# A four-layer graph network on one core: the second edge stage split in two, its larger part woven into the deep passes

## The chip, the cores and the metric

The kernel runs on one core of a Trainium2 chip. The metric is the device time of one execution in microseconds (us). The engines are TensorE (PE, with its weight loads PEld), VectorE (DVE), ScalarE (ACT), GpSimd (POOL) and SyncE (SP). Each has its own program, and they meet in semaphores. All gathers and scatters by index are issued by POOL; plain transfers are issued by SP or ACT.

## The reference

A graph has 100,000 nodes with 48 features and 50,000 edges, sorted by their destination `dst`. Four layers follow one another, each with a residual and a layernorm.

```python
x = _layernorm(x + L0(x))   # x + segment_sum(relu(x[src] + edge_attr), dst)
x = _layernorm(x + L1(x))   # ten times: f = 0.9 * segment_sum(f[src] * w, dst) + 0.1 * x
x = _layernorm(x + L2(x))   # relu(segment_sum(h2[src, type] * norm, dst) + bias2),
                            #   h2 = relu(x @ W1[r] + b1) @ W2[r], 8 relations r
x = _layernorm(x + L3(x))   # segment_max((x[dst]-x[src]) @ theta.T + theta_b + x[src] @ phi.T + phi_b, dst)
```

All is in float32. A node that no edge points to has a short way of its own, since its sums are zero.

## The kernel before, in words

Edges are worked on in groups of 512 (128 partitions by `T` = 4 columns). There are 100 groups (`NG`), taken four (`U`) to a turn, so 25 turns (`NT`). A running sum over a group of sorted edges is a scan by DVE on transposed data (`tensor_tensor_scan`, with a row of ones and zeros `kb` that restarts it at each new destination). PE makes the transposes.

Ten steps of layer 1 would need ten passes over all edges. The kernel follows chains instead: an edge whose source is nobody's destination ends there. "Level" lists hold the edges that still have a way to go, and they shrink: 40 groups at level 0, 20 at level 1, 10 at level 2. After that seven "deep" passes of ten groups each go on over the last list. Stages run one after the other, with a barrier between them. In the order of the trace they are: setup, counting and clearing, node stage, first edge stage, second edge stage, level 0, level 1, level 2, deep passes, sum stage, third-layer stage, fourth-layer stage.

**Second edge stage.** One group's work ("body") is a row of parts with lags: in step g the engines do layer 1's norm for group g (`norm2`), the relational product of group g−1 (`second`, `weigh` which gives `mw`, and two scans into `sc`: `add_up` and `highest`), layer 2's norm of group g−2 (`norm3`), and the last layer's norm of group g−3 (`norm4`, after the product by `thi` in `own`), whose rows POOL scatters to `out`. `part(work, i, s, lag, end)` places such a part; the order of the calls in a `body` is the order on the engine. The stage also writes `rt` (both scans' rows) into columns of `run_rows`, and SP copies `upper_rows` beside them. While it runs, POOL gathers for 44 of the groups (`listed=True`, 11 turns at most) the rows of parents (`fetch`) that level 0 needs, and SP stores them to `parent_rows`.

**Level 0** (`level(0, run_rows)`) gathers rows of 193 numbers from `run_rows` (the running sum's 97 and `rt`'s 96), computes with the first 97 and stores the other 96 to `held`, from which the third-layer stage reads later.

**Deep passes** (`steps`, function `one`). For each of ten groups: POOL gathers four times 128 rows of the last pass (`ugb`), DVE multiplies by the edge weight (`message`, `umsg`), PE transposes, DVE scans (`add_up`), PE transposes back, ACT copies to `rbuf` (`urb`), DVE adds that to a total kept in SBUF for all groups (`total_2`, printed as `total`), and SP stores `rbuf` for the next pass. In the first pass a second table, `fourth`, is added once. The last pass scales `rbuf` by ten, adds the total and scatters it to `deep_sum`. A pass can start its gathers only when the pass before has stored all of its rows. Engines know only each other's semaphores, so the deep list's count, read from memory, sets the trips of each loop.

**Sum stage.** For the 40 groups of level 0's list it adds `first_sum` and two `deep_sum` tables, does the norm, and stores to `layer[2]`. POOL has no part in it.

## Time and profile before

| | us |
|---|---|
| median of 3 runs | 4377.33 |
| lowest and highest run | 4374.49, 4379.94 |
| span of the profiled execution | 4361.2 |
| second edge stage, by the trace | 1376 to 2400 |
| level 0 | 2405 to 2670 |
| level 1 | 2690 to 2912 |
| level 2 | 2935 to 3005 |
| deep passes | 3010 to 3497 |
| sum stage | 3503 to 3620 |

Busy shares over the whole span are PE 56%, DVE 66%, ACT 31%, POOL 60%. They are means over stages with different limits. All times of instructions below are in us from the start of the span, on the one core. A row of the timeline gives start, duration, engine, line of the kernel, operation, result and operands by the program's names, shape, count, and in brackets the engine's idle time before it and what ended that. A name such as `bank` is a PSUM bank.

### The profile page before, as it was taken

To read this page: it belongs to the slowest core of one execution; us is meant where nothing else is said; L and a number is where in the kernel's file an instruction comes from. 1 tells how busy PE (TensorE), PEld (TensorE's weight loads), DVE (VectorE), ACT (ScalarE), POOL (GpSimd) and SP (SyncE) were. 2 spreads that over 40 slices of the span, in tenths; PEclk is the share of its full clock that TensorE was granted. 3 is DMA by queue.
4 is the path that set the end of the run, shared out by engine and by line. 5 is a ranking of instruction groups with operands and counts; after the bars stand their busy time and mean duration, and the time that the engine had idled before them with its cause. 6 is when DMAs were issued, how large, how long until landed. Compare 5 with 4: busy or idle time off the path is not lost. (4 is left out here: it accounts for less than half of the span.)

```text
span 4361.2 us, 60883 instructions
## 1 busy us (share of the span) xinstructions
PE 2429.7 (56%) x9482; PEld 1156.1 (27%) x9482; DVE 2868.7 (66%) x7411; ACT 1336.2 (31%) x4693; POOL 2603.5 (60%) x2544
## 2 busy tenths in 40 slices
PE   4720000677774888888886675642222106986564
PEld 2510000333331443344443221111111102333332
DVE  7989998788894888788887675323323144663333
ACT  0023333455552554455544221111000013431111
POOL 4747772666663777744444664756556604646776
PEclk9965555799997999899998897775555558995555
DMA  6647776899997866855553785224434242332111
GB/s 225 238 112 215 218 216 193 161 174 180 179 184 111 203 162 161 174 143 145 142 145 93 185 208 122 67 49 64 46 45 49 28 122 73 74 63 42 37 38 25
DMA packets 628412, 557.12 MB, mean 128 GB/s; under 512 B 379089, under 2 KB 548122, under 8 KB 623330
## 3 DMA queue, kind: packets, MB, share of 16 engines
q1 hardware_dynamic: 477606, 418.72, 35.7%
q0 software_dynamic: 90112, 95.44, 15.7%
q10 hardware_dynamic: 60612, 42.15, 4.6%
q14 instruction: 65, 0.53, 0.0%
q8 instruction: 17, 0.28, 0.0%
HBM read 291.63 MB, written 290.82 MB: 134 GB/s over the span
## 5 line engine op out<-in xcount | busy, mean ns | idle before, releaser
L1303 POOL DMA_INDIRECT out<-xob,ob x400 | 414.7, 1037 | 354.8 <-DVE xob L1415 246.8
L487 POOL DMA_INDIRECT xdst<-in_x,dstc x400 | 455.3, 1138 | 224.9 <-issue 135.0
L273 POOL DMA_INDIRECT gb<-nodes,ib x400 | 386.3, 966 | 258.0 <-ACT ib L851 141.6
L257 PE MATMUL bank<-ident,act 128*99 128x128 f32 x400 | 70.2, 302 | 657.9 <-ACT act L888 655.5
L273 POOL DMA_INDIRECT cgb<-layer,ib x160 | 175.4, 1096 | 232.4 <-ACT ib L2194 185.9
L293 PE MATMUL bank<-chosen,rec 128*6 128x512 bf16 x1200 | 309.2, 413 | 0.6 <-ACT packed L879 0.6
L1342 PE MATMUL bank<-hm,w 128*48 128x512 f32 x600 | 294.1, 629 | 0.0
L1359 PE MATMUL bank<-bxT,w 105*128 105x512 f32 x600 | 282.7, 607 | 8.5 <-ACT bxT L1246 8.5
L267 PE MATMUL bank<-ident,scan 99*128 99x99 f32 (+2 forms) x1120 | 200.2, 309 | 136.2 <-DVE scan L2013 101.5
L286 PE MATMUL bank<-l_chosen,l_rec 128*3 128x512 f32 x480 | 254.0, 679 | 0.5 <-DVE l_chosen L280 0.3
L273 POOL DMA_INDIRECT parent<-upper_rows,ib x176 | 175.3, 996 | 121.6 <-ACT ib L1271 57.1
L267 PEld LDWEIGHTS bank<-ident,scan 99*128 99x128 f32 (+2 forms) x1120 | 156.9, 212 | 297.8 <-issue 297.8
L257 PEld LDWEIGHTS bank<-ident,act 128*99 128x99 f32 x400 | 51.5, 179 | 669.7 <-issue 669.6
L273 POOL DMA_INDIRECT l_gr<-run_rows,ib x160 | 166.2, 1039 | 92.9 <-issue 43.3
L257 PE MATMUL bank<-ident,umsg 128*48 128x128 f32 x280 | 71.4, 410 | 260.7 <-DVE umsg L2003 260.7
L273 POOL DMA_INDIRECT ugb<-edges,ib x160 | 152.3, 952 | 105.8 <-issue 83.7
L564 PE MATMUL bank<-hot_at,hot_no 128*125 128x400 f16 x800 | 155.5, 338 | 95.6 <-DVE hot_at L590 95.6
L273 POOL DMA_INDIRECT dgb<-layer,ib x160 | 156.7, 979 | 81.4 <-issue 47.9
L2003 DVE TENSOR_TENSOR umsg<-ugb,w 128x192 f32<-128x192 f32 x70 | 25.1, 359 | 268.5 <-DMA ugb<-edges,ib 169.0
L2422 POOL DMA_INDIRECT out<-xo,dob x160 | 160.0, 1000 | 54.7 <-issue 47.6
L1235 ACT ACTIVATE bq_<-bd_ 128x192 f32<-128x192 f32 x300 | 98.3, 359 | 299.3 <-DVE bd_ L1402 244.5
L257 PE MATMUL bank<-ident,l_msg 128*99 128x128 f32 (+1 forms) x280 | 58.6, 345 | 228.9 <-DVE l_msg L1779 228.9
(293 smaller groups left out, 6920.3 us busy)
## 6 DMA issues: line engine op xcount, KB each, us to landing
nodes<-wt SPq DMA_DIRECT2D x40, 1286.2 KB
edges<-gb ACTq DMA_DIRECT2D x100, 194.0 KB
upper_rows<-tb SPq DMA_DIRECT2D x100, 194.0 KB
xa<-upper_rows SPq DMA_DIRECT2D x100, 194.0 KB
lsb<-edges SPq DMA_DIRECT2D x100, 194.0 KB
run_rows<-upper_rows SPq DMA_DIRECT2D x100, 194.0 KB
deep_sum<-zeros SPq DMA_DIRECT2D x20, 960.0 KB
layer<-zeros SPq DMA_DIRECT2D x20, 960.0 KB
```

Source lines behind the costliest of these rows:

```text
L257: last = nc.tensor.transpose(slot(dst_ps[0:w, :], t), rows_sb[:, t, c0:c0 + w], ident[:, :])
L267: last = nc.tensor.transpose(dst_ps[:, t, 0:w], slot(cols_sb[0:w, :], t), ident[0:w, 0:w])
L273: yield nc.gpsimd.indirect_dma_start(out=dst[s][:, t, 0:width], out_offset=None, in_=table, in_offset=bass.IndirectOffsetOnAxis(ap=ib[s][: ...
L286: last = nc.tensor.matmul(ps[0:w, :], rec[:, t, :], chosen[:, t, :], start=t == 0, stop=t == T - 1)
L293: last = nc.tensor.matmul(ps[0:w, :], rec[:, k, t, :], chosen[:, t, :], start=t == 0 and k == 0, stop=t == T - 1 and k == K3 - 1)
L487: nc.gpsimd.indirect_dma_start(out=xdst[:, k * F:(k + 1) * F], out_offset=None, in_=a["x"], in_offset=bass.IndirectOffsetOnAxis(ap=dstc[:, ...
L564: last = nc.tensor.matmul(psC[h], hot_no[b][:, t, 0:HP], hot_at[b][:, t, h * HALF:(h + 1) * HALF], start=first and t == 0, stop=final and ...
L1235: nc.scalar.activation(q[:, :, :], d[:, :, :], ACT.Square).then_inc(s_sq[k], 1)
L1303: nc.gpsimd.indirect_dma_start(out=out, out_offset=bass.IndirectOffsetOnAxis(ap=ob[s][:, t:t + 1], axis=0), in_=xo[s][:, t, :], in_offset= ...
L1342: last = nc.tensor.matmul(psM[0:F, :], w2[:, q, :], hm[b][q][:, :], start=q == 0, stop=q == RC - 1)
L1359: nc.tensor.matmul(psH[q][:, :], w1[:, q * P:(q + 1) * P], xT[s][:, :], start=True, stop=True).then_inc(s_h, 1)
L2422: nc.gpsimd.indirect_dma_start(out=out, out_offset=bass.IndirectOffsetOnAxis(ap=ob[s][:, t:t + 1], axis=0), in_=xo[s][:, t, :], in_offset= ...
```

## The change

- The second edge stage becomes a function, `second_stage(scope, tag, lo, turns_n, psH, carried)`, used twice. The first use ("b_") does 11 turns (`FIRST`), 44 groups, as a stage of its own. The second ("e_") does the other 56 groups inside `steps`. Both share the scans' buffer `sc`, whose last column carries the running sums over. The second use has two PSUM banks for the hidden products where the first has three.
- In each deep pass the engines' programs are: two edge bodies, then six steps in which one deep group and one edge body are interleaved, then a loop over the remaining four deep groups without edge work. Seven passes by eight bodies are 56 groups. After the last pass three steps drain the edge pipeline. POOL scatters an edge group four bodies after its start, not three.
- The deep passes now follow Horner's rule. `rbuf` is the pass's sum plus the term of the first pass, read back from DRAM (`third`, `fourth`); the last addition scales by ten. There is no `total_2` and no copy by ACT. PSUM goes from two banks each for the two transposes to one each (`psT`, `psR`). The keep rows, the added term and the stores of the deep passes are issued by ACT's queue, not SP's. POOL gathers at most two groups ahead, not four.
- Parents are gathered beside the bodies for eight turns, and for a ninth after the drain (`rest`).
- `rt` goes to a table of its own (`rt_rows`). Level 0 gathers 97 wide from `upper_rows` and stores no `held`; it keeps its indices (`idxr`). In the sum stage POOL gathers 96 wide from `rt_rows` for its 40 groups, and SP stores `held` there.
- The parents' rows have one more table in the rotation of the levels; it is cleared in the counting stage with 21 more transfers of 960 KB.

The core of the diff (the bodies' parts themselves only moved into `second_stage`):

```diff
+FIRST = 11
+        rt_rows = dram("rt_rows", (EP + 1, 2 * F))
+        parents = dram("parents", (fills * P * ZW,))
+        level_rows = [rows_in(nodes, PW), rows_in(parents, PW), rows_in(nodes, F)]
+        swap_rows = [rows_in(nodes, F), rows_in(parents, F)]
+                    for z in parents.rearrange("(k q w) -> k q w", q=P, w=ZW):
+                        sp.dma_start(z, zeros[:, :]).then_inc(s_clear, 16)
...
+        def second_stage(scope, tag, lo, turns_n, psH, carried):
@@ second_stage, SP @@
+                def body(i, s, end=None):
+                    part(load, i, s, 0, end)
+                    part(store_x2, i, s, 3, end)
+                    part(store_rt, i, s, 4, end)
+                    part(store_x3, i, s, 5, end)
...
@@ second_stage, PE @@
+                def head(i, s, end=None, between=None):
+                    part(columns, i, s, 0, end)
+                    part(second, i, s, 1, end)
+                    if between is not None:
+                        between()
+                    part(cols_d, i, s, 3, end)
+                    part(first, i, s, 0, end)
+                def tail(i, s, end=None):
+                    part(own, i, s, 3, end)
+                    part(sums, i, s, 1, end)
...
@@ second_stage, DVE @@
+                def head(i, s, end=None):
+                    part(norm2, i, s, 0, end)
+                    part(weigh, i, s, 1, end)
+                    part(add_up, i, s, 1, end)
+                    part(lambda *z: spread_of(2, *z), i, s, 0, end)
+                    part(highest, i, s, 1, end)
+                    part(norm2_end, i, s, 0, end)
+                def tail(i, s, end=None):
+                    part(norm4, i, s, 3, end)
+                    part(add_bias, i, s, 1, end)
...
-                        sp.dma_start(run_rows[bass.ds(g * GE + 1, GE), 0:PW], upper_rows[bass.ds(g * GE + 1, GE), :]).then_inc(s_cp[s], 16)
...
@@ level 0 @@
-                                sp.wait_ge(s_g[s], (i + 1) * 16 * gathers)
-                                sp.dma_start(held[bass.ds(g * GE, GE), :].rearrange("(p t) f -> p t f", t=T), gr[s][:, :, PW:TW]).then_inc(s_sgw[s], 16)
-        level(0, run_rows)
+        level(0, upper_rows)
...
@@ deep passes, PE @@
+                            for s in range(2):
+                                head(2 * k, s)
+                                tail(2 * k, s)
+                            for j in range(3):
+                                for s in range(2):
+                                    turn, b = 2 * k + (j * 2 + s + 2) // U, (j * 2 + s + 2) % U
+                                    head(turn, b, between=lambda: columns(j, s))
+                                    sums(j, s)
+                                    tail(turn, b)
+                            with pe.Fori(3, n) as i:
+                                for s in range(2):
+                                    columns(i, s)
+                                    sums(i, s)
@@ deep passes, DVE: the addition, and the woven step @@
+                                nc.vector.scalar_tensor_tensor(out=rbuf[s][:, :, :], in0=psR[:, :, :], scalar=float(STEPS) if mode == "ten" else 1.0, in1=ad[s][:, :, :], op0=ALU.mult, op1=ALU.add).then_inc(s_acc, 1)
+                                    begin(j, s)
+                                    head(turn, b)
+                                    add_up(j, s)
+                                    tail(turn, b)
@@ deep passes, ACT @@
+                                    load(j, s)
+                                    body(2 * k + (j * 2 + s + 2) // U, (j * 2 + s + 2) % U)
+                                    listed(j, s)
...
@@ sum stage, SP and POOL @@
+                        sp.dma_start(rows(held, i * U + s), flat(hr[s])).then_inc(s_hw[s], 16)
+                        for ins in gather(s, rt_rows, hr, 2 * F):
+                            ins.then_inc(s_g[s], 16)
```

On PE, one step of the second edge stage before, up to the transposes of the last layer's rows:

```order
L1366 MATMUL bank<-thi,dT 128x48 x4
L267 MATMUL bank<-ident,sc 128x112 x4
L257 MATMUL bank<-ident,lsb 96x128 x4
L1336 REGISTER_ALU
L1340 MATMUL bank<-bxT,pmt 48x512
L1342 MATMUL bank<-hm,w 48x512 x3
L262 MATMUL bank<-ident,x3d 48x128 x4
```

And on PE, one woven step now (names that begin with `e_` are the edge body's; `umsg` and `scan` are the deep group's):

```order
L1283 MATMUL bank<-e_bxT,pmt 48x512
L1285 MATMUL bank<-e_hm,w 48x512 x3
L266 MATMUL bank<-ident,umsg 48x128 x4
L271 MATMUL bank<-ident,e_x3d 48x128 x4
L1302 MATMUL bank<-e_bxT,w 128x512 x3
L276 MATMUL bank<-ident,scan 128x48 x4
L1309 MATMUL bank<-thi,e_dT 128x48 x4
L276 MATMUL bank<-ident,sc 128x112 x4
L266 MATMUL bank<-ident,e_lsb 96x128 x4
```

The deep group's first transposes stand behind the second product, and its second transposes (of `scan`) stand between the first product (L1302) and the product by `thi` (L1309, before L1366).

On DVE, the part of a step around the two scans and the start of the last layer's norm, before:

```order
L1433 TENSOR_TENSOR mw<-bank,nb 48x512
L1442 SCALAR_TENSOR_TENSOR sc<-kb,sc,mw 48x512
L1408 TENSOR_REDUCE bu_<-bq_ 128x4
L1451 SCALAR_TENSOR_TENSOR sc<-kp,sc,bank 48x512
L1414 RECIPROCAL br_<-bs_ 128x4
L1415 TENSOR_TENSOR x2d<-bd_,br_ 128x192
L1477 TENSOR_TENSOR by_<-bank,rt 128x192
```

And on DVE in a woven step now:

```order
L2114 TENSOR_TENSOR umsg<-ugb,w 128x192
L2127 SCALAR_TENSOR_TENSOR urb<-bank,uad 128x192
L1368 SCALAR_TENSOR_TENSOR e_bd_<-e_xa 128x192
L1369 SCALAR_TENSOR_TENSOR e_own_row<-e_xa,far 128x4
L1379 TENSOR_TENSOR e_mw<-bank,e_nb 48x512
L1388 SCALAR_TENSOR_TENSOR sc<-kb,sc,e_mw 48x512
L1354 TENSOR_REDUCE e_bu_<-e_bq_ 128x4
L1397 SCALAR_TENSOR_TENSOR sc<-e_kp,sc,bank 48x512
L1360 RECIPROCAL e_br_<-e_bs_ 128x4
L1361 TENSOR_TENSOR e_x2d<-e_bd_,e_br_ 128x192
L2136 SCALAR_TENSOR_TENSOR scan<-ukl,scan,bank 48x512
L1423 TENSOR_TENSOR e_by_<-bank,e_rt 128x192
```

The message and the previous group's addition open the step; the deep scan stands between the head's last instruction (`x2d`) and the tail's first (L1423, before L1477), which reads the product by `thi`.

## Rows read from the trace of the kernel before

**Rows 1.** The page, its first line.

```profile
span 4361.2 us, 60883 instructions
```

**Rows 2.** Windows: length, busy us (count) of PE, PEld, DVE, ACT, POOL, PEclk, DMA, GB/s.

```profile
756.00:1372.00 616.00, 436.04 (x2000) 206.97 (x2000) 501.23 (x1713) 308.10 (x1802) 386.32 (x400) 0.89 0.97 169
1840.00:2395.00 555.00, 465.44 (x1935) 227.16 (x1933) 477.18 (x1269) 270.60 (x685) 251.04 (x247) 0.97 0.50 134
2705.00:2912.00 207.00, 131.99 (x316) 39.98 (x316) 79.14 (x218) 29.62 (x154) 158.35 (x153) 0.77 0.31 63
3084.00:3150.00 66.00, 18.05 (x84) 10.82 (x84) 20.92 (x33) 5.62 (x23) 40.35 (x43) 0.50 0.40 47
```

**Rows 3.** Timeline, one step of the second edge stage, PE and DVE.

```profile
2103.70 0.36 DVE L1422 SCALAR_TENSOR_TENSOR bd_<-xa 128x192 f32<-128x192 f32 x1 [0.21 <-issue]
...
2106.33 1.09 PE L1366 MATMUL bank<-thi,dT 50*128 50x48 f32 x8
...
2107.88 0.71 PE L267 MATMUL bank<-ident,sc 112*128 112x112 f32 x4 [0.46 <-issue]
...
2108.41 0.36 DVE L1477 TENSOR_TENSOR by_<-bank,rt 128x192 f32<-128x192 f32 x1
2108.43 0.60 PE L257 MATMUL bank<-ident,lsb 128*96 128x128 f32 x4
...
2113.13 0.35 DVE L1422 SCALAR_TENSOR_TENSOR bd_<-xa 128x192 f32<-128x192 f32 x1
```

**Rows 4.** One line's instructions: duration ns min/median/max, first and last start.

```profile
L1451 DVE TENSOR_TENSOR_SCAN sc<-kp,sc,bank x99: 1285/1286/1287, 1425.9 to 2369.0; 48x512 f32<-48x512 f32 x99
...
L273 POOL DMA_INDIRECT ugb<-edges,ib x160: 942/947/1129, 3010.3 to 3475.7; - x160
```

**Rows 5.** Groups by line, deep passes: busy us, mean ns, idle before, its enders.

```profile
L2013 DVE TENSOR_TENSOR_SCAN scan<-kb,scan,bank 48x512 f32<-48x512 f32 x63 | 80.1, 1272 | 56.4 <-PE bank L257 56.4
L2003 DVE TENSOR_TENSOR umsg<-ugb,w 128x192 f32<-128x192 f32 x70 | 25.1, 359 | 268.5 <-DMA ugb<-edges,ib 169.0 <-DMA ugb<-nodes,ib 99.5
```

**Rows 6.** Timeline, end of one deep pass and start of the next.

```profile
3128.93 0.36 DVE L2003 TENSOR_TENSOR umsg<-ugb,w 128x192 f32<-128x192 f32 x1 [3.91 <-DMA ugb<-nodes,ib]
...
3133.05 0.36 DVE L1996 TENSOR_TENSOR total<-total,urb 128x192 f32 x1 [1.29 <-ACT urb L1897]
...
3135.73 0.95 POOL L273 DMA_INDIRECT ugb<-edges,ib  x1 [13.15 <-issue]
3136.98 0.95 POOL L273 DMA_INDIRECT ugb<-edges,ib  x1 [0.30 <-issue]
...
3142.59 0.36 DVE L2003 TENSOR_TENSOR umsg<-ugb,w 128x192 f32<-128x192 f32 x1 [9.18 <-DMA ugb<-edges,ib]
```

**Rows 7.** Groups by line, second edge stage, 1440 to 1820: the parents' gathers.

```profile
L273 POOL DMA_INDIRECT parent<-upper_rows,ib x140 | 140.7, 1005 | 42.7 <-issue 42.7
```

**Rows 8.** Timeline of PE, its start into the second edge stage.

```profile
1406.73 1.06 PE L257 MATMUL bank<-ident,lsb 128*96 128x128 f32 x4 [19.21 <-DMA lsb<-edges]
...
1412.22 2.84 PE L1359 MATMUL bank<-bxT,w 105*128 105x512 f32 x6
```

**Rows 9.** Timeline of POOL, the last scatter of the second edge stage.

```profile
2393.87 0.98 POOL L1303 DMA_INDIRECT out<-xob,ob  x1 [0.30 <-issue]
```

**Rows 10.** Timeline, first load of the sum stage and first write after it.

```profile
3503.39 0.36 SPq L2072 DMA_DIRECT2D myb<-first_sum  x1
...
3620.31 0.48 DVE L2286 MEMSET xT<- 32x512 f32 x1 [4.45 <-PEq L96]
```

**Rows 11.** Groups by line, level 0, 2460 to 2660.

```profile
L273 POOL DMA_INDIRECT l_gr<-run_rows,ib x124 | 129.3, 1043 | 65.2 <-issue 33.6 <-DMA held<-l_gr 30.8 <-ACT l_rec L1649 0.9
...
L1776 DVE SCALAR_TENSOR_TENSOR l_y<-l_gr 128x192 f32<-128x192 f32 x31 | 11.2, 362 | 28.0 <-DMA first_sum<-l_y 27.9
```

**Rows 12.** Windows, two stretches of the counting stage.

```profile
150.00:160.00 10.00, 7.81 (x42) 5.17 (x41) 10.00 (x27) 0.97 (x5) 7.56 (x9) 1.00 1.02 405
230.00:240.00 10.00, 7.89 (x42) 5.26 (x43) 10.00 (x26) 1.17 (x6) 0.00 (x0) 1.00 0.00 0
```

## What the change should do to the time

> **What bounds the kernel now.** I read the page's first line, then busy time by stage, then inside the two stages that are merged. The profiled execution spans 4361.2 us [rows 1]; the median of the runs is 4377.3, so 16.1 us lie around the span and I keep them. The kernel is a string of stages with different limits, so no engine's share says much; each stage must be priced alone. In the second edge stage DVE is busy 477 of 555 us and PE 465, at a granted clock of 0.97, while in a deep pass DVE is busy 21 of 66 us, PE 18, and the granted clock is 0.50 [rows 2]. That contrast is the whole idea: the passes have idle DVE and PE, the edge stage has work for them.
>
> The edge stage runs at one group per 9.43 us (L1422 at 2103.70 and again at 2113.13) [rows 3]. DVE sets this: within the step the product by `thi` (L1366, 1.09 us) starts at 2106.33 and is over before DVE wants it at 2108.41, so PE costs nothing. Over all groups the scans run from 1425.9 to 2369.0 [rows 4]: 98 steps, 943 us; at 9.43 for the last 58, the first 40, in which parents are fetched too and the pipeline fills, take (943 − 547) / 40 = 9.9.
>
> A deep group costs DVE a message (0.36) and a scan (1.27) [rows 5] and an addition (0.36 at 3133.05 [rows 6]), 2.0 us, but it cannot recur faster than POOL issues its four gathers, 4 × (0.95 + 0.30) = 5.0 us. A pass ends with a chain: last message to end of the last addition 4.5 us (3128.93 to 3133.41), and the next starts with one: first gather to first message 6.9 (3135.73 to 3142.59) [rows 6]. A pass takes 66 to 67 us for ten groups; ten messages, scans and additions are 20.
>
> **What goes.** 56 edge groups leave the stage: 56 × 9.43 = 528, and 8 groups are no longer slowed by the parents' gathers, 8 × 0.5 = 4. Together **−532**. POOL needs more than DVE in the groups that also fetch parents (8 DMAs of 1.0 + 0.3 us, 10.5 [rows 7], against 9.9); after 32 of them it is some 20 us late, and the 12 groups without fetches, which cost it 5.2 of 9.4 us each, make that good. The copy of `upper_rows` into `run_rows` hid on SP and is worth nothing.
>
> **The woven step.** A step of edge body plus deep group on DVE is: message 0.36, previous addition 0.36, edge head 4.71 (2103.70 to 2108.41), deep scan 1.27, edge tail 4.72 [rows 3, 5], 11.4 in all. But the order puts PE's four transposes of the deep scan ahead of the product by `thi`, and DVE's next instruction after the deep scan is the first of the tail, `by` from `psTh` (L1477 before, L1423 now), which reads that product. So DVE now waits, in every woven step, for transposes (0.55: 2107.88 to 2108.43) and product (1.09) and two handovers of 0.1: **1.85 us**, 13.3 in all. Queued behind that wait are DVE's whole tail and the next message; nothing else waits earlier. ScalarE's new index copy and three DMA issues come between its last root of one step and its copy of `xT` in the next, where PE is not yet ready for it. POOL's four gathers and four scatters, 10.5 us, are covered, and it may run two groups ahead. At the lower clock the two pieces double and the step is 14.4; bounds 11.4 and 14.4 plus the rival below. First edge stage and level 1 have PE busy 0.71 and 0.64 of the time and a granted clock of 0.89 and 0.77 [rows 2]; the woven step has 7.9 (465/555 of 9.43) + 1.2 for the two sets of deep transposes, 9.1 of 13.3 = 0.68. I take half way, **13.8**.
>
> The Trainium skill (TensorE: Matmul & The Clock Gate, Loop structure matters more than you think) says that a long wait between matmuls drops the clock while dense work keeps it. By it every stretch of deep groups without an edge body starts cold, and a wait inside the woven step may too; the trace agrees for the passes (0.50). By the rule alone every woven step would be 14.4, 19 to 22 us more over all passes.
>
> **A pass.** It has ten deep groups: two edge bodies ahead of them, six woven steps, four deep groups alone.
> Entry: PE comes out of the lone groups at the low clock, and its transposes and second product take 5.5 us from 1406.73 to 1412.22 [rows 8]; DVE waits 5.1, then does the rest of the head from `mw` on (4.3) and, after a wait of 0.3, the tail (4.7): 14.4. The second body 9.4. Sum 23.8. The new pass's first gathers wait for the last store (about 2.5) and for POOL's two scatters, and land some 10.5 us in, so they are hidden.
> Woven: 12.9 (no addition yet) + 5 × 13.8 = 81.9.
> Alone: groups 7 and 8 have their gathers already, 3.7 us each; group 9's gathers start with group 7's message and land 6.9 later; group 10's 5.0 to 5.5 after; then the closing 4.5 [rows 6]. 17.5, bounds 16.6 and 20.
> **P = 123.2.** The first pass, from its first gather, 115 (empty pipeline: no tail yet, but cold products). The last pass adds scatters of its own: POOL then issues 10 gathers, 10 deep scatters and 12 edge scatters in groups of four, 128 × 1.30 = 166, + 2 to land = 168, against 161 on DVE's side: P, 5 for the second addition of each group, and a drain of 33, of which 26 are seen before (last scan 2369.0 [rows 4] to last scatter 2394.9 [rows 9]). So 115 + 5 × 123.2 + 168 + 9 of barrier = 908, where first gather to next stage was 3503.4 − 3010.3 = 493 [rows 4, 10]. **+415.**
>
> The Trainium skill (SBUF — State Buffer, Who interferes with whom) says that GpSimd and some DVE instructions exclude each other. The gathers average 1.00 us beside the busy DVE [rows 7] and 0.95 in the passes [rows 6]: it agrees and is small. By it the last pass would be 168 to 175.
>
> **The rest.** Parents: eight turns are fetched beside the 44 groups, the last turn's 16 gathers come after the last scatter [rows 9], 16 × 1.3 + landing and store, where now only two stores follow: **+22**, nothing hides it. Bounds 18 and 27.
> Sum stage: 3503.39 to 3620.31, 117 us, with POOL empty [rows 10]. 160 gathers at 1.27 are 203, + 12 for the first index, the last landing, its store and the barrier: 215, **+98**. Bounds: 1.25 to 1.33 each, +95 to +110; below +95 only if gathers overlapped, which POOL's rows never show.
> Level 0: the store of `held` goes. Its issue stands on SP ahead of the store for which DVE waits at `l_y` (27.9 us in 31 groups), and POOL waits 30.8 for it [rows 11]. A step takes 200/32 = 6.25 us; with both waits gone it could fall by 0.9, to 5.4, where POOL's four gathers (1.04 + 0.30) are late next. I take 0.65 for 38 groups, **−25**, bounds 0 and −34. Level 2 loses an addition and a copy and gains a store: −2.
> Clearing `parents`: 21 × 0.98 MB at 405 GB/s, 51 us. The clearing now ends near 170 and the stage at 262 with its DMAs idle [rows 12]: free.
>
> Sum: −532 + 415 + 22 + 98 − 25 − 2 = **−24**: span 4337, time **4353**.
>
> **Rivals.** *Clean weave:* if the product by `thi` is not waited for, steps cost 11.4; six passes gain 6 × 13.5 = 81, the last is POOL's: 4272. Against it stands the order; for it, little. *Slower: the clock.* All PE work of a woven step, 9.1 us at 2.4 GHz, is up to 18.2 at 1.2. If its wait of some 2.6 us for the deep scan (first product over 4.2 us into the step, deep scan at 6.8) leaves PE at the low level for most of each step, PE becomes the bound; with steps of 16 P is 136.5, six passes +80: 4433. It decides from 14.5 us a step, where the 24 us are gone. For it: level 1's 0.77, and 17 quiet us per pass; against: the first edge stage's 0.89 at the same share. (It is the Trainium skill's rule on waits, named above, at its harshest.) *Lone groups:* the gathers land as in the steady pass, 9.5 after their start, and the handover shows; 3 us more in each of seven passes, 4374: no change.
>
> **Numbers.** Forecast 0.50, clean weave 0.12, clock 0.25, lone groups 0.13. The runs before differ by 5.5 us; about 0.2% (8.8 us) can be told from no change. Forecast's own range from steps of 13.3 to 14.4, level 0 and gather bounds: 4325 to 4388; it gives 0.36 faster, 0.11 same, 0.03 slower; clean weave 0.12 faster; clock 0.24 slower, 0.01 same; lone groups 0.03, 0.07, 0.03. Faster 0.51, same 0.19, slower 0.30. The range 4295 to 4425 leaves out most of the clean weave and the worst of the clock.
>
> **What would show it.** Woven steps of 13.3 to 14.4 between successive `umsg` with an edge body, DVE idle before L1423 of 1.8 us put down to L1309's product; passes of 123 us; 17 to 18 between the last woven body and the next pass's body; the last pass bound by POOL; sum stage 215; about 22 of POOL alone before level 0; level 0 steps at 5.6; the counting stage unchanged. Wrong if L1423 does not wait, if the granted clock in the woven steps is near 0.5, or if messages wait for gathers there.

## The result, and the profile after

The changed kernel takes 4392.56 us (median of 5 runs, 4389.72 to 4402.44), and the kernel before, on the same chip, 4377.33 (4370.97 to 4379.94). The ratio is 1.0045, 95% interval 1.0033 to 1.0056: slower by 15 to 20 us, where 24 us faster was forecast. The time lies inside the range that was given, 4295 to 4425, but on the other side of no change.

The page's first line after, for [rows 1]:

```profile
span 4387.9 us, 59752 instructions
```

This execution was timed at 4389.72, so a run lies 1.8 us above its span, not 16.1. The trace of before (4361.2) was thus an execution some 14 us shorter than the median run, and shorter than the lowest of its five runs. The record doesn't say on which chip it was taken, nor on which the result was measured; the chips of the later runs it numbers 10, 15 and 8.

So before was traced once more, on chip 10, where its median is 4355.7 (before_again, one run of 4357.57). The expectation put the missing time into DMA-bound stages ahead of the second edge stage or into that stage; its rival put it into the deep passes or level 0, and then the table below would overstate what the change does there. The rival falls: the second trace spans 4355.5, and in every row of the table it agrees with the first within 2.1 us (level 0 285.6, deep passes 493.7). On chips 15 and 8 the medians of before are 4398.0 and 4398.8. The trace of copy_late on chip 15, a kernel as fast as before there, is 40 us longer than chip 10's, and 30 of these are in the first edge stage. Ratios below are therefore to before on the same chip, and stages are compared by differences within a trace.

What the two traces say by stage comes from one line's answer, the gathers by their first and last start. Before (answers to [rows 4]; the third and fourth rows are levels 1 and 2):

```profile
L273 POOL DMA_INDIRECT parent<-upper_rows,ib x176: 942/969/1599, 1382.0 to 1826.3; - x176
L273 POOL DMA_INDIRECT l_gr<-run_rows,ib x160: 943/950/1345, 2411.8 to 2653.0; - x160
...
L273 POOL DMA_INDIRECT l_gp<-edges,ib x80: 943/948/2041, 2695.7 to 2887.4; - x80
L273 POOL DMA_INDIRECT l_gp<-nodes,ib x40: 942/947/1247, 2938.3 to 2991.8; - x40
```

After:

```profile
L282 POOL DMA_INDIRECT parent<-upper_rows,ib x160: 938/966/1858, 1395.7 to 1878.1; - x160
L282 POOL DMA_INDIRECT l_gr<-upper_rows,ib x160: 940/974/1308, 1899.2 to 2115.8; - x160
L282 POOL DMA_INDIRECT ugb<-nodes,ib x160: 940/947/1891, 2473.1 to 3379.3; - x160
L282 POOL DMA_INDIRECT mhr<-rt_rows,ib x160: 940/944/1118, 3437.4 to 3636.6; - x160
...
L282 POOL DMA_INDIRECT l_gp<-nodes,ib x80: 940/946/1247, 2161.1 to 2350.5; - x80
L282 POOL DMA_INDIRECT l_gp<-parents,ib x40: 940/944/1257, 2400.3 to 2453.7; - x40
```

| from, to | before | after | difference | forecast |
|---|---|---|---|---|
| start, first parent gather | 1382.0 | 1395.7 | +13.7 | 0 |
| to level 0's first gather | 1029.8 | 503.5 | −526.3 | −510 (−532 + 22) |
| level 0 | 283.9 | 261.9 | −22.0 | −25 |
| levels 1 and 2 | 314.6 | 312.0 | −2.6 | −2 |
| deep passes (after: with 56 edge groups), to the sum stage's first load | 493.1 | 963.4 | +470.3 | +415 |
| sum stage | 116.9 | 211.8 | +94.9 | +98 |
| the rest | 740.9 | 739.6 | −1.3 | 0 |

The sum stage's first load and the first write after it, for [rows 10]:

```profile
3436.50 0.35 SPq L2218 DMA_DIRECT2D myb<-first_sum  x1
...
3648.34 0.48 DVE L2462 MEMSET xT<- 32x512 f32 x1 [15.99 <-PEq L97]
```

The columns add up to the 26.7 us between the spans; 13.7 of them come ahead of the second edge stage. The added clearing is not among them: the first edge stage's first gather is at 767.3 before and at 768.6 after, so it was free, as forecast.

The merged stage is 55 us over its forecast, and that is more than all of the miss. Windows of one pass after, the six woven steps and the four lone groups (columns of [rows 2]):

```profile
2751.00:2831.00 80.00, 62.18 (x240) 32.51 (x240) 60.51 (x150) 30.99 (x78) 41.34 (x42) 0.82 0.43 114
2831.00:2857.00 26.00, 7.55 (x36) 4.77 (x36) 8.37 (x15) 0.77 (x4) 19.23 (x20) 0.50 0.66 88
```

The woven steps are 13.3 us each here (13.4 over passes 0 to 5), at a granted clock of 0.82. One of them, on DVE:

```profile
2817.07 0.35 DVE L2114 TENSOR_TENSOR umsg<-ugb,w 128x192 f32<-128x192 f32 x1
...
2822.32 1.27 DVE L2136 TENSOR_TENSOR_SCAN scan<-ukl,scan,bank 48x512 f32<-48x512 f32 x1
...
2826.18 0.36 DVE L1423 TENSOR_TENSOR e_by_<-bank,e_rt 128x192 f32<-128x192 f32 x1 [2.58 <-PE bank L1309]
```

The scan ends at 2823.59, and then DVE waits 2.58 us for the product by `thi` (L1309). In other steps it waits 1.73. The wait stands where the order of PE's work put it, and its two sizes are the two levels of PE's clock. The product by `thi` in a step with the short wait (it ends at 2798.72), and in the step above:

```profile
2797.62 1.05 PE L1309 MATMUL bank<-thi,e_dT 50*128 50x48 f32 x8
...
2824.23 1.91 PE L1309 MATMUL bank<-thi,e_dT 50*128 50x48 f32 x8
```

The windows from the deep scan's end to DVE's next instruction in these two steps (the third number from the end is the granted clock):

```profile
2796.90:2798.70 1.80, 1.57 (x13) 1.54 (x13) 0.09 (x1) 0.00 (x0) 1.25 (x2) 1.00 0.28 90
2823.60:2826.10 2.50, 2.36 (x13) 2.30 (x13) 0.00 (x0) 0.00 (x0) 0.00 (x0) 0.50 0.17 56
```

In the second, third and fourth pass of this trace, steps with the long wait take 13.6 to 14.3 us and the others 12.4 to 13.3. So the mean of 0.82 is made of stretches at full and at half clock.

The four lone groups, on ScalarE, POOL and DVE:

```profile
2830.10 0.19 ACT L1953 COPY ib<-idx 128x4 int32<-128x4 int32 x1
2831.11 0.94 POOL L282 DMA_INDIRECT ugb<-nodes,ib  x1 [8.97 <-ACT ib L1953]
2831.15 0.36 DVE L2114 TENSOR_TENSOR umsg<-ugb,w 128x192 f32<-128x192 f32 x1
...
2836.10 0.94 POOL L282 DMA_INDIRECT ugb<-nodes,ib  x1 [0.31 <-issue]
2838.29 0.36 DVE L2114 TENSOR_TENSOR umsg<-ugb,w 128x192 f32<-128x192 f32 x1 [3.58 <-DMA ugb<-nodes,ib]
2841.09 0.94 POOL L282 DMA_INDIRECT ugb<-nodes,ib  x1 [0.30 <-issue]
2844.84 0.94 POOL L282 DMA_INDIRECT ugb<-nodes,ib  x1 [0.30 <-issue]
2846.63 0.36 DVE L2114 TENSOR_TENSOR umsg<-ugb,w 128x192 f32<-128x192 f32 x1 [5.50 <-DMA ugb<-nodes,ib]
2852.56 0.40 DVE L2114 TENSOR_TENSOR umsg<-ugb,w 128x192 f32<-128x192 f32 x1 [3.10 <-DMA ugb<-nodes,ib]
2856.76 0.35 DVE L1368 SCALAR_TENSOR_TENSOR e_bd_<-e_xa 128x192 f32<-128x192 f32 x1
```

The seventh group's message is at 2831.15. The eighth group's gathers begin at the same moment (2831.11), after POOL waited 8.97 us for the index, which ScalarE copied only when the edge body was through. The ninth group's gathers are issued from 2836.10 to 2841, and its message comes at 2846.63; the tenth's are issued by 2845.78, and its message comes at 2852.56. From the seventh message to the next pass's first edge instruction (2856.76) it is 25.6 us, over passes 0 to 5 25.9 in the mean, where 17.5 was forecast.

### The profile page after: what moved, and what is told of

Read it like the earlier page. It is cut to its first block and busy times, and to the rows that moved or that the text cites. A ratio compares the mean times of both kernels' runs of the same rounds, so it can differ in the third digit from the quotient of the medians.

```text
span 4387.9 us, 59752 instructions
## 1 busy us (share of the span) xinstructions
PE 2507.7 (57%) x9482; PEld 1192.0 (27%) x9482; DVE 2866.6 (65%) x7406; ACT 1336.5 (30%) x4703; POOL 2744.2 (63%) x2688
## 5 line engine op out<-in xcount | busy, mean ns | idle before, releaser
L1255 POOL DMA_INDIRECT out<-e_xob,e_ob x224 | 226.4, 1011 | 105.8 <-issue 65.5
L282 POOL DMA_INDIRECT ugb<-nodes,ib x160 | 157.1, 982 | 182.1 <-ACT ib L1953 96.5
L1255 POOL DMA_INDIRECT out<-b_xob,b_ob x176 | 186.4, 1059 | 80.6 <-issue 51.4
L282 POOL DMA_INDIRECT parent<-upper_rows,ib x160 | 160.5, 1003 | 108.3 <-ACT ib L1535 60.4
L1285 PE MATMUL bank<-e_hm,w 128*48 128x512 f32 x336 | 213.0, 785 | 0.0
L282 POOL DMA_INDIRECT l_gr<-upper_rows,ib x160 | 165.7, 1036 | 72.0 <-issue 46.0
L282 POOL DMA_INDIRECT ugb<-parents,ib x120 | 117.5, 979 | 125.7 <-ACT ib L1953 83.8
L282 POOL DMA_INDIRECT mhr<-rt_rows,ib x160 | 151.7, 948 | 63.5 <-issue 40.5
L1302 PE MATMUL bank<-e_bxT,w 105*128 105x512 f32 x336 | 170.7, 628 | 0.8 <-ACT e_bxT L1210 0.8
```

Source lines behind the costliest of these rows:

```text
L282: yield nc.gpsimd.indirect_dma_start(out=dst[s][:, t, 0:width], out_offset=None, in_=table, in_offset=bass.IndirectOffsetOnAxis(ap=ib[s][: ...
L1255: nc.gpsimd.indirect_dma_start(out=out, out_offset=bass.IndirectOffsetOnAxis(ap=ob[s][:, t:t + 1], axis=0), in_=xo[s][:, t, :], in_offset= ...
L1285: last = nc.tensor.matmul(psM[0:F, :], w2[:, q, :], hm[b][q][:, :], start=q == 0, stop=q == RC - 1)
L1302: nc.tensor.matmul(psH[(s * RC + q) % HB if HB < RC else q][:, :], w1[:, q * P:(q + 1) * P], xT[s][:, :], start=True, stop=True).then_inc( ...
```

## The experiments

All ratios are to the kernel before on the same chip, with their 95% interval. Each experiment ran on one chip: early_index, own_first and both_moved on 10, unwoven, edge_loads_late, held_split and copy_late on 15, the others on 8. Where two of them on different chips are compared, it is by their ratios, or by stages of their traces. Gains against the change are reckoned from its 1.0045; from its 1.0036 on chip 8 each is 4 us less. "Merged stage" is from the first deep gather to the sum stage's first gather, 964.3 us in the trace above.

**The change once more, on chip 8.**

> The change as it is, once more, on this chip: ratio 1.003 to 1.006 as before. Its first trace spent 14 us more than its siblings in the first edge stage, which the change doesn't touch; theory: that is spread from one execution or chip to the next, and here the stage ends where it ends in the other traces of this chip, with passes of 129 to 130 us and a merged stage of 960 to 966 us unchanged.

Measured: 4414.07 against 4398.84, ratio 1.0036 (1.0023 to 1.0048). Merged stage 965.9, passes 1 to 5 127.0 to 132.5, 129.6 in the mean. The first edge stage's last gather is at 1355.1, in the other traces of chips 8 and 15 at 1355 to 1360, and in those of chip 10 at 1321 to 1328, with the changed and the unchanged kernel alike. So the change doesn't lengthen that stage. The trace of before has 1327.5, as on chip 10, and the trace after has 1342.3: that the 13.7 us of the table's first row are a difference of chips is likely, but not shown, since the record doesn't name the chips of these two.

**Two moves in the woven step.** The first moves ScalarE's index copy, the second PE's product by `thi`.

```diff
 # ACT, woven step (early_index)
                                     load(j, s)
+                                    stage(j + 1, s)
                                     body(2 * k + (j * 2 + s + 2) // U, (j * 2 + s + 2) % U)
-                                    listed(j, s)
+                                    listed(j, s, staged=True)
 # PE, woven step (own_first); tail is own, between(), sums
-                                    sums(j, s)
-                                    tail(turn, b)
+                                    tail(turn, b, between=lambda: sums(j, s))
```

> The change, with one thing moved: in the six woven steps of a deep pass ScalarE copies the index for the gathers two groups on ahead of the edge body, not behind it. Theory (late index): after the last woven message the four lone groups take 26 us where 17.5 was forecast, since the eighth group's gathers start only when the edge body is through; with the copy moved they start one step sooner, the lone part falls from 26 to about 20 us in each of seven passes, and the time by 35 to 45 us, to about 4350. Rival (slow landing): the gathers of the lone groups land late because the transfers of the next edge groups share the DMA engines; then the copy's place is worth little, the eighth group's message comes sooner but the tenth's does not, and the time falls by less than 12 us. The woven steps stay at 13.3 us by both.

Measured: ratio 0.9972 (0.9961 to 0.9982), 0.73% below the change's 1.0045: 32 us. Merged stage 941.6, 23 below. That is less than the 35 to 45 of the theory and more than the 12 of its rival. The lone part is 21.7 to 25.0, mean 22.8, not 20. In the pass that answers to the one above:

```profile
2788.46 0.95 POOL L282 DMA_INDIRECT ugb<-nodes,ib  x1 [3.56 <-ACT ib L1953]
...
2801.85 0.94 POOL L282 DMA_INDIRECT ugb<-nodes,ib  x1 [8.52 <-ACT ib L1953]
```

```profile
2800.25 0.36 DVE L2116 TENSOR_TENSOR umsg<-ugb,w 128x192 f32<-128x192 f32 x1
...
2803.80 0.33 DVE L2116 TENSOR_TENSOR umsg<-ugb,w 128x192 f32<-128x192 f32 x1
...
2812.55 0.36 DVE L2116 TENSOR_TENSOR umsg<-ugb,w 128x192 f32<-128x192 f32 x1 [5.57 <-DMA ugb<-nodes,ib]
...
2818.23 0.36 DVE L2116 TENSOR_TENSOR umsg<-ugb,w 128x192 f32<-128x192 f32 x1 [2.84 <-DMA ugb<-nodes,ib]
```

The eighth group's gathers now begin at 2788.46, in the last woven step, and its message follows the seventh's at once (3.5 us). But the ninth and tenth messages are still 8.8 and 5.7 us behind. 3.1 of the 8.4 us by which the lone part exceeds its forecast were the late index; the rest is something else.

> The change, with one thing moved: in a woven step PE does the product by thi ahead of the deep group's second transposes, not behind them. Theory (PE order): DVE's idle time ahead of the first instruction of the tail (1.73 or 2.58 us in each woven step of the trace, 104 us in all) goes, a woven step falls from 13.3 to about 11.3 us, and the time by 75 to 95 us, to about 4305. Rival (another bound stands right behind): POOL has eight DMAs a step, 10.5 us with the gaps, and ScalarE's index copies come after the edge body, so DVE then waits for gathers; the step falls only to 12.5 or more and the time by less than 40 us.

Measured: ratio 0.9891 (0.9875 to 0.9908), 1.5% or 67 us below the change. Woven steps are 11.8 us. Merged stage 903.9, 60 below. What DVE waited for ahead of the tail, in the change and then here (us, times):

```profile
  PE bank L1309: 103.8, 48
```

```profile
  PE bank L1309: 18.0, 9
```

The 36 woven steps of passes 0 to 5, 13.4 before the move, give 55 of the merged stage's 60. The gain is under the 75 expected since the last pass's woven steps don't get shorter (85.5 us against 85.1), as POOL has deep scatters there too: at the ends of its last three woven steps DVE waits 4.4, 4.2 and 3.2 us for gathers. Nor does POOL bind in the other passes: the step is 11.8, near the 11.4 that DVE's work alone was counted at. With the wait gone PE is at full clock more of the time, 0.89 in the woven steps of the third pass, where the change has 0.82:

```profile
2707.00:2777.00 70.00, 57.59 (x240) 29.58 (x240) 60.10 (x149) 30.99 (x78) 41.32 (x42) 0.89 0.47 130
```

> Both moves together. If they act on different parts of a pass (late index on the lone groups, PE order on the woven steps), their gains add: 110 to 140 us below the change, about 4265. If POOL is the bound of the woven step once DVE no longer waits, the index moved ahead is worth more here than alone, since gathers can then start sooner in each step: 130 to 150. If the gains are the same time counted twice, the sum is under 100.

Measured: ratio 0.9846 (0.9829 to 0.9862), 87 us below the change; merged stage 885.2, 79 below. The single gains in the merged stage are 23 and 60, 83 together, so they add to within 4 us. By the ratios it is 87 against 32 and 67. Taken by its number alone, under 100 is the third case of the expectation (the same time counted twice), but that limit came from single gains which had been forecast too high, and the merged stage doesn't bear it out.

**Is it the edge traffic that makes the last gathers land late?**

```diff
 # SP, merged stage
+                                    if i == 0 and s == 3:
+                                        sp.wait_ge(s_msg, k * m)
...
```

> Both moves, and SP holds back the loads of each pass's last prefetched edge group (about 0.6 MB: upper rows, edge rows, keep rows) until the pass's last deep message. Theory (slow landing): these transfers fill the DMA engines while the lone groups' gathers should land, so without them the spacing of the ninth and tenth message falls from 8.9 and 5.9 us to about 5 to 6 each and the lone part from 22 to 18 or 19: 15 to 25 us off both_moved. Rival (the gathers' own queue is the limit, or ScalarE's own transfers): no change in the spacing, within 6 us of both_moved.

Measured: ratio 0.9853 (0.9838 to 0.9868), no gain over both_moved (0.9846); the spacings of the last two messages stay 8.7 to 9.0 and 6.2 to 6.8. The edit did move the loads: in the third pass of both_moved two of the group's six (L1153, L1155) were issued at 2783.4 and 2784.1, with the seventh message, and here they come at 2836.7 and 2837.3, after the tenth. The other four wait in both traces until the next pass. So this theory falls.

**The passes without edge bodies.** `FIRST = 25`; all calls of the second use's parts are taken out of `steps`.

> The change without the weave: FIRST is 25, so all 100 edge groups stand in the stage of their own, and the deep passes (Horner, keep rows, added term and stores on ScalarE's queue, one PSUM bank for each transpose) run without edge bodies. Everything else is as in the change. Theory (the passes' new form costs nothing by itself): a pass takes 66 to 70 us as before, and against the kernel before the time is +23 (parents' tail) +95 (sum stage) -22 (level 0) -15 (first groups of the edge stage without the copy) = +75 to +100, about 4440 where before is 4356. Rival (the new form slows the lone groups: the load of ScalarE's queue, one bank each): the lone groups are as far apart as in the change, 7 to 8 us, a pass takes 80 us or more, and the time is above before by 170 or more.

Measured: ratio 1.0165 (1.0149 to 1.018), +72 us, just under the 75 to 100 of the first theory and far from the 170 of its rival. Merged stage (now deep passes alone) 502.8. First message to next first message of a pass is 64.6 us in the mean over passes 0 to 5 against 63.3 in the trace of before: the new form costs about 1.3 us a pass. It also shows the late landing with no edge work beside it:

```profile
3121.91 0.36 DVE L2080 TENSOR_TENSOR umsg<-ugb,w 128x192 f32<-128x192 f32 x1 [2.31 <-DMA ugb<-parents,ib]
...
3130.04 0.36 DVE L2080 TENSOR_TENSOR umsg<-ugb,w 128x192 f32<-128x192 f32 x1 [5.29 <-DMA ugb<-parents,ib]
...
3136.41 0.36 DVE L2080 TENSOR_TENSOR umsg<-ugb,w 128x192 f32<-128x192 f32 x1 [3.54 <-DMA ugb<-parents,ib]
```

```profile
3124.85 0.94 POOL L282 DMA_INDIRECT ugb<-parents,ib  x1 [0.31 <-issue]
...
3128.60 0.94 POOL L282 DMA_INDIRECT ugb<-parents,ib  x1 [0.30 <-issue]
```

These are the last three messages of the pass, and the last gathers of its ninth and tenth group. POOL issues without a pause until 3129.5, and the messages up to the eighth are 4.6 to 5.3 us apart. The ninth is 8.1 behind the eighth, the tenth 6.4 behind the ninth, 6.9 us after its last gather was issued. Before showed it too: at the end of the pass in [rows 6] the last three messages are at 3114.86, 3122.09 and 3128.93.

**One hot row.** The deep list of these inputs has 4103 entries, 8.01 groups of 512, and a pass works on an even number of groups. So the ninth group has 7 real entries and the tenth none, and padded entries gather row 0. The edit gives each padded entry (its weight `w_2` is zero) a row of its own.

```diff
+  # once, after level 2 (other is a float tile; idxr holds rows spread over the table)
+  nc.vector.scalar_tensor_tensor(out=other, in0=w_2, scalar=0.0, in1=idxr, op0=ALU.is_equal, op1=ALU.mult)
+  nc.vector.tensor_tensor(idx3, idx3, other, ALU.add)
```

> Both moves, and after level 2 two VectorE instructions give each padded entry of the deep list (weight zero) a row of its own to gather, where all padded entries gathered row 0. The list has 4103 entries, 8.01 groups of 512, so of the ten groups a pass works on the ninth has 7 real entries and the tenth none. Theory (one hot row): the ninth and tenth group's gathers land 5.5 to 7 us after the last of them is issued, where others land in 2.2 to 2.5, with or without edge work beside them, because all 512 read one row; spread, the spacings of the last two messages fall from 8.9 and 5.9 to about 7 and 5, the lone part from 22.3 to 17 or 18, and the time by 25 to 35 us, to a ratio of about 0.977. Rival (the last gathers of a run land late whatever they read, since nothing is queued behind them or stores lie in the way): no change, within 5 us of both_moved.

Measured: ratio 0.9784 (0.9767 to 0.98), 0.6% or 27 us below both_moved's 0.9846 on the other chip; merged stage 857.6, 27.6 below. The end of the pass:

```profile
2811.16 0.36 DVE L2127 TENSOR_TENSOR umsg<-ugb,w 128x192 f32<-128x192 f32 x1
2814.68 0.33 DVE L2127 TENSOR_TENSOR umsg<-ugb,w 128x192 f32<-128x192 f32 x1
2820.37 0.36 DVE L2127 TENSOR_TENSOR umsg<-ugb,w 128x192 f32<-128x192 f32 x1 [2.49 <-DMA ugb<-nodes,ib]
2825.25 0.36 DVE L2127 TENSOR_TENSOR umsg<-ugb,w 128x192 f32<-128x192 f32 x1 [2.04 <-DMA ugb<-nodes,ib]
2829.41 0.35 DVE L1370 SCALAR_TENSOR_TENSOR e_bd_<-e_xa 128x192 f32<-128x192 f32 x1
```

5.7 and 4.9 us where there were 8.8 and 5.7, and 18.3 from the seventh message to the next pass. Over passes 0 to 5 the lone part is 18.8.

> The kernel before with the same spreading of padded entries alone. Theory (hot row): in a pass of the trace of before the last two messages are 7.2 and 6.8 us behind their forerunners where the others are 5.0; they fall to 5.0, a pass from 66.6 to about 62.5, and the time by 25 to 30 us (ratio 0.994). Rival (end of the run): no change.

Measured: ratio 0.9941 (0.9924 to 0.9958), and a pass of 59.5 us in the mean, from first message to first message, where it is 63.3 in the trace of before. At the end of its second pass the messages are 5 us apart to the last:

```profile
3145.77 0.36 DVE L2015 TENSOR_TENSOR umsg<-ugb,w 128x192 f32<-128x192 f32 x1 [2.23 <-DMA ugb<-nodes,ib]
3150.69 0.36 DVE L2015 TENSOR_TENSOR umsg<-ugb,w 128x192 f32<-128x192 f32 x1 [2.08 <-DMA ugb<-nodes,ib]
3155.78 0.36 DVE L2015 TENSOR_TENSOR umsg<-ugb,w 128x192 f32<-128x192 f32 x1 [2.16 <-DMA ugb<-nodes,ib]
```

In the pass after this one the ninth message is still 7.4 us behind, but there POOL issued its gathers 2.7 us later than in the others, and they landed nearly as fast. The hot row is shown in both kernels, by edits that change only what padded entries read.

**Where the held rows are gathered.**

```diff
 # third-layer stage, POOL, slots 2 and 3 (held_split) or slot 3 alone (all_in)
                         for ins in gather(s, layer[2], gb, F):
                             ins.then_inc(s_g[s], 16)
+                        if s >= 2:
...
+                            for ins in gather(s, rt_rows, chr_, 2 * F, T):
+                                ins.then_inc(s_hg[s], 16)
```

> Both moves, and the gathers of held rows are shared: half of the groups (slots 0 and 1 of each turn) in the sum stage, the other half in the third-layer stage, where POOL gathers them straight into the tile that VectorE adds, and SP stores them for the last stage. Theory (each of the two stages has idle POOL time: the sum stage took 117 us without gathers, the third-layer stage is 307 us with 200 of POOL): 80 gathers are 100 us, so the sum stage falls from 212 to about 125, and the third-layer stage, POOL 300 of 307, grows by 0 to 12: 75 to 87 us off both_moved, about 4205. Rival (POOL's gathers in the third-layer stage are on its path, by the wait for an index or the landing): it grows by 40 or more, and under 50 us are won.

Measured: ratio 0.9764 (0.9749 to 0.9779), 36 us below both_moved, not 75: the rival's number. Against both_moved the sum stage fell by 81, but the third-layer stage rose from 307 to 347. The groups by line there, 3530 to 3830:

```profile
L282 POOL DMA_INDIRECT cgb<-layer,ib x147 | 152.3, 1036 | 44.8 <-issue 44.8
...
L282 POOL DMA_INDIRECT chr<-rt_rows,ib x76 | 79.8, 1050 | 23.3 <-issue 23.3
```

232 us busy and 68 us of gaps in 300, all of them issue: POOL is full at 1.34 us a gather, and 240 of them are 322. I had reckoned with 1.25. What binds is this rate, not a wait for an index or a landing, which the rival had named.

**All together:** both moves, the spread, and the held rows of one group in four in the third-layer stage.

> Both moves, the spread, and the held rows gathered for three groups of four in the sum stage and for one of four in the third-layer stage. Theory: in held_split the third-layer stage had 240 gathers at 1.34 us, 322 us, and grew by 40; with 200 it has 268 and stays near 307, while the sum stage has 120 gathers, 150 + 13 = 163 where both_moved has 217. So 50 us off both_moved from the split and 25 to 35 from the spread: a ratio to before of about 0.966. Rival: gathers in the third-layer stage hold up the next group's gathers, and it grows by 15 or more: 0.970 or above.

Measured: 4252.35 us against 4398.84, ratio 0.9667 (0.9651 to 0.9684), the fastest of all, as expected (0.966). Sum stage 166.7, third-layer stage 308.5, merged stage 860.8.

**The copy of `upper_rows`.**

```diff
-                        part(copy_upper, i, s, 0, end)
+                        part(copy_upper, i, s, 3, end)
```

> The kernel before with one thing moved: SP issues the copy of upper_rows into run_rows three groups later, so that in the first groups of the second edge stage the loads come first. Theory: the copies stand ahead of the loads when the pipeline fills (in two traces of before 33 to 35 us from the first parent gather to the first scan, in the changed kernels 18 to 21), so the time falls by 10 to 15 us, 0.3%. Rival: the wait for the first edge rows is for the writes of the stage before, whatever stands in the queue: no change (within 4 us).

Measured: ratio 0.9998 (0.9989 to 1.0007). The theory's 10 to 15 us don't come. The first ten groups of the second edge stage take 117.8 us, 118.5 and 119.6 in the two traces of before, and 102 to 106 in the kernels without the copy. So its place in the queue isn't what costs; whether its traffic is, or the strided store of `rt` into the same rows, was not tried.

## Why the prediction was wrong

**What goes (−532 forecast, with the parents' tail −510; measured −526).** The tail is as counted: from the last scatter's issue to level 0's first gather 41 us, where before it is 18 [rows 9]. The groups that stay are faster than counted, where 4 us had been given to them. Against the trace of before the first ten take 14 us less in the trace after and in the change once more, and 16 in unwoven; the next 33 take 5 less in the first of these and 9 to 11 in the other two. That parents are now fetched beside eight turns and not eleven is a reason for the second gain that no run tests. "The copy hid on SP and is worth nothing" was said without a row for the fill, and a part of this gain may be the copy: copy_late rules out only its place in the queue.

**The woven step (13.8 forecast, 13.4 measured).** The wait behind the deep transposes was found where the order put it, at 1.73 and 2.58 us against 1.85 counted, and own_first shows that it is the order: 67 us. The two sizes are the product and its transposes at full and at half clock. The forecast for a step all at the low level, 14.4, is a wrong sum: with both pieces doubled (1.10 and 2.18) and the handovers it is 14.9. It did no harm, since such steps took 13.6 to 14.3, and 13.8 as half way between the levels was a guess that came out near.

The Trainium skill (TensorE: Matmul & The Clock Gate, Loop structure matters more than you think) says that PE goes cold when a long wait stands between its matmuls. The trace agrees in the lone groups (0.50). In the woven steps it shows both levels (0.82 in the mean). The clock rival would have had steps of 14.5 or more. It falls: 13.4 with the wait, 11.8 without.

**The entry (23.8 forecast, 23.4 measured for passes 1 to 5)** was right; DVE waits 4.8 us for the second product in the pass after the one above, where 5.1 was counted.

**The lone groups (17.5 forecast, 25.9 measured): the step that failed.** "Groups 7 and 8 have their gathers already" and the landing of the last two groups' gathers, "6.9 later" and "5.0 to 5.5 after", are wrong. Group 8's gathers stood behind an index copy that ScalarE makes after the edge body, one step too late: 3.1 us a pass by early_index (25.9 to 22.8). And groups 9 and 10 are padding that reads one row: another 4.0 (22.8 in both_moved, 18.8 in spread). With both gone the lone part is 18.8, inside the 16.6 to 20 that were given. 8.4 us in each of passes 0 to 5 are 50 of the 55 us by which the merged stage is over its forecast. The last pass adds 15, and woven steps and entries, 1.7 and 0.4 us a pass below their forecast, give 10 or so back.

The prediction counted ScalarE's new instructions between two edge steps and asked whether they hold up `xT`; it did not ask who waits for the index copy among them. The rival "lone groups" named the place, but priced it at 3 us a pass, from a steady pass, when in passes 0 to 5 of before the last two messages were 6.7 to 8.6 and 6.1 to 6.8 us behind their forerunners. The end of a pass was in [rows 6], but only its last message was used. "A pass takes 66 to 67 us" was misread too: from first gather to first gather passes 0 to 5 take 62.4 to 64.9. No term of the sum rests on that.

**The last pass (177 with the barrier forecast, 192 measured).** POOL was rightly named as what binds it, but it is longer than POOL's 168 since POOL also waits: 6.1 us for the finished rows of an edge group (`e_xob`) in the entry, and 6.0 for an index copy in the woven steps. What own_first saves in the woven steps of the other passes it doesn't save here.

**Level 0 (−25, measured −22), level 2, the sum stage (+98, measured +94.9, a hair under its bound of 95)** were right. POOL sets the sum stage, as this group for 3440 to 3640 shows, 150 us busy and 48 idle in 200, of which 40 are its own issue gaps and 7.6 a wait for the store of `held`:

```profile
L282 POOL DMA_INDIRECT mhr<-rt_rows,ib x158 | 149.8, 948 | 48.2 <-issue 40.2 <-DMA held<-mhr 7.6 <-ACT ib L2259 0.3
```

**Around the span.** 16.1 us were put around the span where 1.8 are. The forecast's difference of −24 doesn't depend on it.

Where the gain went, then: the weave by itself is worth 1.2 to 1.3% (unwoven 1.0165 against 1.0036 and 1.0045, about 55 us), and what comes with it costs more: held rows gathered by POOL in the sum stage, 95, and the parents' tail, 23, less 22 of level 0 and 20 to 25 of the edge stage's first 44 groups. That is 71 to 76 us, and unwoven, which has all of it and no weave, is 72 slower than before. One correction to the section on the change: POOL gathers at most two groups ahead in the deep passes of both kernels; "not four" was mistaken.

## What to carry to other kernels

When two programs are woven, write down for each small instruction who waits for it, on every engine, and look at its place in the woven step; here one copy of 0.2 us and one matmul group in the wrong place cost 23 and 60 us of the merged stage. Price the end of a loop by the rows of its end, not by its steady part. And ask what padded entries read: if it is one row, spread them.

## What the runs showed of the hardware

- A deep group gathers 512 rows with four instructions. When all are one and the same row (the tenth group, passes 0 to 5), its message starts 5.2 to 7.8 us after the last instruction's end, over the traces of all kernels that leave padded entries on row 0. In the three kernels that spread them (spread, before_spread, all_in) it is 1.6 to 2.3. POOL issues at the same 1.25 us in both.
- The kernel before has medians of 4356 us on chip 10, 4398 on 15 and 4399 on 8, and 4377 where the result was measured. Most of the difference sits in the first edge stage, where the DMA engines are busy 0.97 of the time [rows 2]: its last gather starts at 1326.6 on chip 10 (before_again) and at 1357.5 on 15 (copy_late), its first at 767.8 and 768.8.
- The same wait of DVE for PE comes in two sizes within one pass, 1.73 us where the granted clock during the wait is 1.00 and 2.58 where it is 0.50; the eight matmuls of the product take 1.05 and 1.91. The mean over the pass's woven steps is 0.82, and 0.89 when the order of PE's work no longer makes DVE wait.
